# Attention pair scaling: where the inverse sums are transposed and who multiplies them in

## What is computed

```
scores = einsum('ehd,ehd->eh', q[tgt], k[srcidx])
m = segment_max(scores, tgt);  p = exp(scores - m[tgt])
s = segment_sum(p, tgt)
w = p / (s[tgt] + 1e-16)
agg = segment_sum(w[:, :, None] * v[srcidx], tgt)
```

## Time and profile before

| | |
|---|---|
| median of 3 runs | 2668.23 us (2665.0 to 2670.25) |
| the profiled execution | 2664.81 us |
| its span, first to last instruction | 2663.1 us |
| TensorE busy | 2443.1 us (92%) |
| VectorE busy | 2082.2 us (78%) |
| ScalarE busy | 1736.8 us (65%) |
| GpSimd busy | 1067.5 us (40%) |
| mean granted TensorE clock | 0.966 |

### The profile page before, as it was taken

One profiled execution on the slowest core, in us unless ns is written; L12 is line 12 of the kernel. 1 busy time (PEld: TensorE's weight loads), 2 busy tenths in 40 slices (PEclk: granted clock), 3 DMA queues, 4 the chain that ended last, 5 costly groups with the idle time before them and its releaser, 6 DMA issues. The chain is left out here.

```text
span 2663.1 us, 44829 instructions
## 1 busy us (share of the span) xinstructions
PE 2443.1 (92%) x12851; PEld 1940.1 (73%) x12851; DVE 2082.2 (78%) x4185; ACT 1736.8 (65%) x3839; POOL 1067.5 (40%) x1037
## 2 busy tenths in 40 slices
PE   6999799998998999989999998798999999986887
PEld 3777555555797999957799995466777777765776
DVE  8789799999645889835498884656999999865757
ACT  2789888887734777714377772242999999835560
POOL 1456655544302544100144420114777777700312
PEclk9999899999999999999899999898999999988999
DMA  2004022213044444112444441114877777822101
GB/s 92 2 2 124 15 65 68 65 52 99 27 192 114 120 117 114 38 64 99 135 119 116 92 76 63 48 66 130 246 239 238 238 237 239 202 58 63 53 8 40
DMA packets 115827, 278.08 MB, mean 104 GB/s; under 512 B 23271, under 2 KB 37546, under 8 KB 115694
## 3 DMA queue, kind: packets, MB, share of 16 engines
q0 software_dynamic: 50560, 138.73, 19.4%
q1 hardware_dynamic: 65134, 137.65, 16.6%
HBM read 208.80 MB, written 59.38 MB: 101 GB/s over the span
## 5 line engine op out<-in xcount | busy, mean ns | idle before, releaser
L803 POOL DMA_INDIRECT feature_rows<-in_edge_attr,id_idx x352 | 340.6, 967 | 447.1 <-POOLq L1504 224.9
L2078 POOL DMA_INDIRECT x_got<-table_dram,src_idx x352 | 374.9, 1065 | 110.0 <-issue 82.9
L1438 DVE TENSOR_TENSOR pt_low<-bank,pt_high 128x640 fp32r<-128x640 f32 x320 | 262.9, 822 | 52.1 <-ACT pt_high L1401 50.9
L758 ACT ACTIVATE hot_rest<-hot_dst,slot_w 128x128 bf16<-128x128 bf16 x864 | 273.0, 400 | 46.0 <-DVE hot_dst L708 44.1
L1401 ACT CAST pt_high<-bank 128x640 fp32r<-128x640 f32 x320 | 219.6, 687 | 113.7 <-PE bank L1352 113.6
L2222 DVE TENSOR_TENSOR msg<-bank,x_got 128x512 f32<-128x512 f32 x352 | 237.2, 685 | 44.1 <-ACT msg_high L2167 15.7
L1432 DVE CUSTOM_DVE_ANT_0 p<-bank,log_counts 128x1254 f32<-128x1254 f32 x160 | 232.7, 1455 | 15.0 <-PE bank L1335 15.0
L1352 PE MATMUL bank<-ident,p 128*128 128x128 f32 x1600 | 228.4, 274 | 2.3 <-DVE pt_low L1438 2.3
L1393 ACT ACTIVATE p<-p,bound 128x1254 f32<-128x1254 f32 x160 | 215.4, 1346 | 10.0 <-DVE bound L1432 10.0
L1363 PE MATMUL bank<-pt_high,val 128*128 128x256 f32 x800 | 212.4, 300 | 0.9 <-DVE agg_t L1444 0.9
L2202 DVE SCALAR_TENSOR_TENSOR msg_low<-msg,msg_high 128x512 fp32r<-128x512 f32 x308 | 210.4, 684 | 0.0
(11 more groups left out here) (435 smaller groups left out, 6404.0 us busy)
## 6 DMA issues: line engine op xcount, KB each, us to landing
features_dram<-feature_rows POOLq DMA_DIRECT2D x88, 256.0 KB
edge_got<-features_dram SPq DMA_DIRECT2D x88, 256.0 KB
qk_dram<-qk_high SPq DMA_DIRECT2D x16, 640.0 KB, 2.9
qk_dram<-qk_low SPq DMA_DIRECT2D x16, 640.0 KB, 4.2
keys<-qk_dram SPq DMA_DIRECT2D x32, 320.0 KB, 4.9
queries<-qk_dram SPq DMA_DIRECT2D x32, 320.0 KB, 6.7
queries_low<-qk_dram SPq DMA_DIRECT2D x32, 320.0 KB, 9.0
acc_a<-zeros SPq DMA_DIRECT2D x1, 6400.0 KB
```

What stands on the lines that cost most here:

```text
L758: last = act.activation(hot_rest[:, u, j, q, :], hot_dst[:, u, :, j], ACT.Copy, scale=k.slot_w[:, 1 + q, bass.ds(tile0 + j, 1)])
L803: pool.indirect_dma_start(out=self.rows[:, u, t % GT * ED:(t % GT + 1) * ED], out_offset=None, in_=self.a.edge_attr_128, in_offset=bass.In ...
L1438: dve.tensor_tensor(p_low[:, made % 3, :, columns], unit(2 * n + u).rearrange("p (j n) -> p j n", n=P), p_high[:, made % 3, :, columns].bi ...
L2078: pool.indirect_dma_start(out=xg[:, g % XRING, j, :], out_offset=None, in_=k.table_dram, in_offset=bass.IndirectOffsetOnAxis(ap=k.src_idx[ ...
```

## The change

For the first three pairs, the inverses no longer go through the place of the scores.

- `turn_plan` lists the units in order: the p units as before, and after the second unit of blocks 24, 44 and 64 and of blocks 25, 45 and 65 one unit more, with half of a pair's inverses each (`turn_inverse`, five transposes). The ring of two units runs through this list, so that each unit waits for the item two places before it in the list.
- `copy_inverse` on ScalarE, after `exp(n + 2)` of the same steps, copies the unit (128 by 640) to `inv_rows` in SBUF.
- GpSimd multiplies `agg` by `inv_rows` (128 by 1280, both in SBUF). It does so between groups of the gather: after 10, 21 and 27 of the 28 groups of a layer, as `SCALED_BEHIND` works out with `first` moved on each time. It waits there for both copies and for the pair's last `add`. `copy_inverse` of the next pair waits for that multiplication.
- `invert` stays where it is. `spread` and `divide` stay for the last pair alone.
- `rest` moves to another place in SBUF, which makes room for `inv_rows`.

```diff
+SCALED_BEHIND = (30, 53, 76)
 def score_plan():
+    return [("scores", n) for n in range(BLOCKS)] + [("spread", HP - 1)]
+SPREAD_BEHIND, INVERTED = 4, 1
+def turn_plan():
     plan = []
     for n in range(BLOCKS):
-        p = (n - (2 * NB + 5)) // (2 * NB)
-        if n >= 2 * NB + 5 and (n - (2 * NB + 5)) % (2 * NB) == 0:
-            plan.append(("spread", p))
-        plan.append(("scores", n))
-    plan.append(("spread", HP - 1))
+        behind = n - 2 * NB - SPREAD_BEHIND
+        for u in range(2):
+            plan.append(("p", n, u))
+            if behind >= 0 and behind % (2 * NB) in (0, 1) and u == 1:
+                plan.append(("inv", behind // (2 * NB), behind % (2 * NB)))
     return plan
...
         def _(pool):
-            features.gather(pool, GATHERED[l], GATHERED[l + 1])
+            first, end = GATHERED[l], GATHERED[l + 1]
+            for pair in range(HP - 1):
+                until = first + (end - first) * SCALED_BEHIND[pair] // BLOCKS
+                features.gather_groups(pool, first, until)
+                first = until
+                pool.wait_ge(inv_copied, 2 * (pair + 1))
+                pool.wait_ge(batch_added, 2 * HALF * (pair + 1))
+                rows = at.agg[:, pair, :]
+                pool.tensor_tensor(rows, rows, inv_rows[:].rearrange("p u n -> p (u n)"), ALU.mult).then_inc(pair_scaled, 1)
+            features.gather_groups(pool, first, end)
+            features.all_stored(pool, end)
...
+            def unit_free(item):
+                i = turn_of[item]
+                if i >= UNITS:
+                    kind, n, u = turns[i - UNITS]
+                    pe.wait_ge(low_made if kind == "p" else inv_copied, 2 * n + u + 1)
...
+            def turn_inverse(pair, u):
+                pe.wait_ge(inv_ready, pair + 1)
+                unit_free(("inv", pair, u))
+                for j in range(HALF):
+                    t = pe.transpose(unit(("inv", pair, u))[:, j * P:(j + 1) * P], spread_inv(pair)[:, u * HALF + j, :], k.ident[:])
+                t.then_inc(turned, 1)
...
             for n in range(steps):
                 if n < BLOCKS:
                     turn(n, 0)
-                if n + AHEAD < BLOCKS:
-                    kind, i = next(following)
-                    if kind == "spread":
-                        spread(i)
-                        kind, i = next(following)
                 if n >= 2:
                     values((n - 2) // 2, n % 2)
                 if n < BLOCKS:
                     turn(n, 1)
                 if n + AHEAD < BLOCKS:
-                    scores(i)
+                    scores(n + AHEAD)
+                if n in inverse_behind:
+                    turn_inverse(*inverse_behind[n])
             spread(HP - 1)
...
+            def copy_inverse(pair, u):
+                act.wait_ge(turned, turn_of["inv", pair, u] + 1)
+                if pair:
+                    act.wait_ge(pair_scaled, pair)
+                act.copy(inv_rows[:, u, :], unit(("inv", pair, u))).then_inc(inv_copied, 1)
...
                 if n + 2 < BLOCKS:
                     exp(n + 2)
+                if n in inverse_behind:
+                    copy_inverse(*inverse_behind[n])
...
-                if n + AHEAD < BLOCKS:
-                    kind, i = next(following)
-                    if kind == "spread":
-                        divide(i)
-                        kind, i = next(following)
```

More of the change, by code:

```diff
@@ L796, in gather, with gather_groups @@
     def gather(self, pool, first, end):
+        self.gather_groups(pool, first, end)
+        self.all_stored(pool, end)
+    def gather_groups(self, pool, first, end):
         for g in range(first, end):
@@ L806, in gather, with all_stored @@
             pool.dma_start(self.k.features_dram[g, :, :], self.rows[:, u, :]).then_inc(self.saved[u], 16)
+    def all_stored(self, pool, end):
         for u in range(FRING):
@@ L1274, in attend @@
     p_high = r.take("pt_high", [P, 3, HALF, 2 * P], F32R)
-    p_low = Region(nc, at.low_tiles_end, k.tail - 4 * KC * NP).take("pt_low", [P, 3, HALF, 2 * P], F32R)
-    rest = r.take("pv_rest", [P, 2 * P], F32)
+    over_low_tiles = Region(nc, at.low_tiles_end, k.tail - 4 * KC * NP)
+    p_low = over_low_tiles.take("pt_low", [P, 3, HALF, 2 * P], F32R)
+    rest = over_low_tiles.take("pv_rest", [P, 2 * P], F32)
     bound = r.take("bound", [P, 4], F32)
@@ L1279, in attend @@
     features.places(nc, r)
+    inv_rows = r.take("inv_rows", [P, 2, HALF * P], F32)
     flat = k.bank[:].rearrange("p b n -> p (b n)")
@@ L1282, in attend @@
     place = {item: i for i, item in enumerate(plan)}
+    turns = turn_plan()
+    turn_of = {item: i for i, item in enumerate(turns)}
     steps = BLOCKS + 2
+    inverse_behind = {turns[i - 1][1]: item[1:] for i, item in enumerate(turns) if item[0] == "inv"}
     def thirds(rows):
@@ L1288, in attend, with unit @@
     UNITS = 2
-    def unit(i):
+    def unit(item):
+        i = turn_of[item]
         return flat[:, (4 + i % UNITS * 2) * 512:(4 + i % UNITS * 2) * 512 + HALF * P]
@@ L1347, in turn @@
                     pe.wait_ge(exp_done, n + 1)
[L1348 to L1350 removed]
+                unit_free(("p", n, u))
                 for j in range(HALF):
[L1352 removed]
+                    t = pe.transpose(unit(("p", n, u))[:, j * P:(j + 1) * P], p[:, n % AHEAD, (u * HALF + j) * P:(u * HALF + j + 1) * P], k.ident[:])
+                t.then_inc(turned, 1)
[4 more added lines that the diff above has]
+                    t = pe.transpose(unit(("inv", pair, u))[:, j * P:(j + 1) * P], spread_inv(pair)[:, u * HALF + j, :], k.ident[:])
                 t.then_inc(turned, 1)
@@ L1365, in values @@
                 x.then_inc(half_done, 1)
-            following = iter(plan)
-            for item in range(AHEAD):
-                scores(next(following)[1])
+            for n in range(AHEAD):
+                scores(n)
             for n in range(steps):
@@ L1396, in high_part @@
             def high_part(n, u):
[L1397 removed]
+                act.wait_ge(turned, turn_of["p", n, u] + 1)
                 made = 2 * (n // 2) + u
@@ L1400, in high_part @@
                     act.wait_ge(half_done, made - 2)
-                act.copy(p_high[:, made % 3, :, n % 2 * P:(n % 2 + 1) * P], unit(2 * n + u).rearrange("p (j n) -> p j n", n=P)).then_inc(high_made, 1)
+                act.copy(p_high[:, made % 3, :, n % 2 * P:(n % 2 + 1) * P], unit(("p", n, u)).rearrange("p (j n) -> p j n", n=P)).then_inc(high_made, 1)
+            def copy_inverse(pair, u):
[3 more added lines that the diff above has]
+                act.copy(inv_rows[:, u, :], unit(("inv", pair, u))).then_inc(inv_copied, 1)
             def copy_rest(m):
@@ L1437, in low_part @@
                 made, columns = 2 * (n // 2) + u, slice(n % 2 * P, (n % 2 + 1) * P)
-                dve.tensor_tensor(p_low[:, made % 3, :, columns], unit(2 * n + u).rearrange("p (j n) -> p j n", n=P),
+                dve.tensor_tensor(p_low[:, made % 3, :, columns], unit(("p", n, u)).rearrange("p (j n) -> p j n", n=P),
                                   p_high[:, made % 3, :, columns].bitcast(F32), ALU.subtract).then_inc(low_made, 1)
@@ L1459, in _ @@
             dve.memset(p[:, :, SCORES:NP], 0.0).then_inc(pads_zeroed, 1)
-            following = iter(plan)
-            for item in range(AHEAD):
-                take(next(following)[1])
+            for n in range(AHEAD):
+                take(n)
             for n in range(steps):
-                if n + AHEAD < BLOCKS:
-                    kind, i = next(following)
-                    if kind == "spread":
-                        divide(i)
-                        kind, i = next(following)
                 if n < BLOCKS:
@@ L1474, in _ @@
                     low_part(n, 1)
-                if n > 1 and n % (2 * NB) == 1:
+                if n > 1 and n % (2 * NB) == INVERTED:
                     invert(n // (2 * NB) - 1)
                 if n + AHEAD < BLOCKS:
-                    take(i)
+                    take(n + AHEAD)
             divide(HP - 1)
```

5 lines of the change are left out of this document (3 added, 2 removed).

## The result

The changed kernel takes 2654.84 us (median of 5 runs, 2653.38 to 2656.04) where the kernel before takes 2668.23: a ratio of 0.9949, with a 95% interval of 0.9939 to 0.996, or 13.4 us less. A second set of runs on another chip gave 2654.13 against 2667.76, 0.9956 (0.9944 to 0.9968). The forecast was 2654.6.

The account below looks back on a forecast made before the run. TensorE sets the attention's 3.43 us beat, VectorE at its heels. Removing 29.2 us at six pair ends and adding back 15.6 wins 13.6 us (7.6 to 18.4): 2668.2 to 2654.6 us, range 2649.8 to 2660.6, 2648 to 2664 with rivals.

Parts of the forecast that it names:

- The whole of a pair's ends, 29.2 us: Attention, both layers: excess over TensorE's beat at six pair ends, 29.2 us, everything the change can win.
- The inversion, 1.1 us: VectorE's inversion, kept at each pair's end, still delays the next scores: 1.1 us per pair, between 0.9 and 1.3.
- The units, 0.9 + 0.6 us: Two inverse units per pair: 0.92 us of TensorE's transposes, plus two waits in the ring of units, 0.6 us.
- the ring's 0.29: TensorE's turn behind an inverse unit waits for the low part, starting 0.29 us after TensorE is free.
- The upper bound of 2.3 us: Units' cost per pair if TensorE's transposes and ScalarE's copies didn't overlap: 2 x (0.46 + 0.69) us, not 1.5.
- ScalarE's copy, nothing: ScalarE's copy of each inverse unit, 0.68 to 0.69 us, lies beside time already counted and adds nothing.
- The clock: TensorE's granted clock stays up at pair ends, where it fell in three of six before, 1.6 us per drop.
- the rival that it blocks VectorE: GpSimd's multiplication blocks VectorE's SBUF reads, 3.0 us in six places: 2659 half hidden, 2672.6 if none; chance 0.06.
- The pause of 12 us: GpSimd in layer 1 waits some 12 us with nothing in flight ahead of its first multiplication.
- the cover of 11 us in layer 1: Layer 1's last gather store still precedes the stage's last multiplication by 11 us, less the store's landing.
- The wait of the next pair's copy for GpSimd: Only the next pair's inverse copy waits for GpSimd's multiplication, 20 steps (69 us) later.
- the rival of the units that cost nothing: Waits in the ring don't show, since low parts come early after the pause: 18 us won, 2650; chance 0.08.

Follow-up runs that it names:

- e7_gather_late: Changed kernel, but GpSimd gathers 5 groups instead of 10 ahead of each layer's first multiplication; 2837.49 us, where the kernel before took 2805.12 on that chip.

## Why the prediction was right

- *The whole of a pair's ends, 29.2 us.* With units and inversion left out, the takes fall to the beat, so nothing else had been in it. Its split was a little off: a drop of the clock costs 1.3 to 1.4 us in the kernel before and not 1.6. The two layers differ by 1.55 us, but 0.27 of this is that takes 24 and 44 of layer 1 come later than the others: VectorE's addition to the sums lasts 0.31 and 0.34 us there, beside one of GpSimd's indirect transfers, and 0.17 elsewhere.
- *The inversion, 1.1 us.* Measured 1.14, gone when it stands in the gaps, though TensorE's wait ahead of the scores was 0.9 to 1.1 us by its modelled ends and not 1.3. As forecast, take 24 is late by 1.3 us and take 25 comes early.
- *The units, 0.9 + 0.6 us.* The sum of 1.5 was right (1.56), its division wrong. I counted TensorE's 0.46 us as lost in any case and the ring's 0.29 on top. One transpose instead of five changes nothing: the whole 0.75 us is the distance from the old start of the turn to the end of the low part that it now waits for, and TensorE's work fits into it. The upper bound of 2.3 us had no ground for the same reason. The lower one was no bound either: it kept 0.9 us for TensorE's work, which isn't what counts.
- *ScalarE's copy, nothing.* Confirmed by the short copy; whole, it takes the 0.68 us forecast.
- *The clock.* It stayed up in all six ends, which is 4.1 us of the win (3 x 1.6 = 4.8 by the forecast's price). That a wait nearly as long as before brings the drop back in three of six ends was shown.
- *GpSimd.* The multiplication at 2.98 us holds nothing up here, and the rival that it blocks VectorE fell for this kernel: the rows beside it are unchanged. The Trainium skill (SBUF — State Buffer, "Who interferes with whom") exempts a VectorE instruction with at most one input in SBUF, outside its two-port modes; the trace agrees, 1.45 and 0.82 us beside a multiplication as elsewhere. I had left out the condition of the modes, and "at most one input" alone isn't enough: in `e7_gather_late` the addition to the sums, with one input, took 1.90 us in place of 0.17 beside a multiplication. The price of this rival was wrong as well: half of 18 us hidden is 2663.6 us and not 2659. The pause of 12 us was measured at 12.0 and 10.7, the cover of 11 us in layer 1 at 11.5. The wait of the next pair's copy for GpSimd I put 69 us away. That counts from the pair's own copies, but the second multiplication comes late, between groups of the gather: in the changed kernel it ends 29 us ahead of the third pair's first copy in both layers, and it binds once it is 37 to 40 us later.
- *Sum.* 29.2 - 15.6 = 13.6 us forecast, 12.9 us by the ruler, 13.4 us by the medians. That the medians hit the forecast to 0.2 us is partly luck: its start was the distance of 3.4 us between one profiled execution and the median, and the executions of the changed kernel reach over 2.7 us. In the rival of the units that cost nothing, 18 us is the win with TensorE's own work still counted; with nothing at all it would be 29.2 - 6 x 1.1 = 22.6.

By the takes, leaving the place of the scores brings some 8.8 of the 12.9 us even where VectorE multiplies, and the multiplication on GpSimd the other 4.1.

## What to carry to other kernels

In a loop that keeps one beat, the distance between the starts of one instruction measures a disturbance to a tenth of a us, in a single profile, where whole runs scatter by some us. An item put into a ring of two buffers cost here the wait for the buffer behind it and not its own work, which was shorter than the wait; where that is so, make such items few rather than short. An engine that takes over work can still hold up the one it relieves, so see which instructions fall beside it. Work that has to go onto an engine without slack belongs in the place where that engine waits for another, cut to the size of the gap.

## What the runs showed of the hardware that wasn't expected

TensorE's granted clock fell in three of the six ends of each kernel with a long wait: 2.69 to 2.85 us in the kernel before, at a cost of 1.3 to 1.4 us each, and 2.58 to 2.72 us with the lengthened inversion, at 1.56 to 1.58 us each. With a wait of 0.84 to 1.37 us by the profile it fell in none of the 48 ends of eight profiles. Which ends it hits isn't explained by these runs: they aren't the same in the two kernels, and within each of them ends with nearly the same wait did and didn't drop (2.69 us in both cases before).

GpSimd's multiplication of 128 by 1280, with both inputs in SBUF, leaves VectorE's instructions alone that read one input from PSUM, and held up one of 0.17 us, from SBUF to SBUF, until it had ended (seen once).
